# Layer 2's first four token tiles are transposed by VectorE and SBUF transfers instead of TensorE

## The reference

```
x = layernorm(x + attn(x))        # layer 1
x = layernorm(x + ffn(x))         # layer 2

attn:  up = x @ up_w.T;  delta = x @ gate_w.T - local_point
       out = up @ local_approx_output.T
       for m in 1..6: out += (exp(m*log|delta| - c[m]) * sign/keep * up) @ fuse_weight[m].T
       out += (silu(x @ ffn_gate_w.T) * (x @ ffn_up_w.T)) @ ffn_down_w.T      # F = 1248
ffn:   h = silu(x @ q(w1).T) * (x @ q(w2).T);  out = h @ q(w3).T              # H = 1376
q(w) = NF4 quantisation and dequantisation in blocks of 64: w / absmax, nearest of 16 codes, * absmax
```

## Time and profile before

| | us |
|---|---|
| median of 3 runs (range) | 411.65 (411.63 to 411.87) |
| profiled execution, whole | 412.71 |
| its span, first to last instruction | 410.8 |
| TensorE busy in it | 401.8 |
| VectorE, GpSimd, ScalarE busy | 325.1, 290.1, 267.4 |

### The profile page before, as it was taken

One profiled execution on the slowest core, in us unless ns is written; L12 is line 12 of the kernel. 1 busy time (PEld: TensorE's weight loads), 2 busy tenths in 40 slices (PEclk: granted clock), 3 DMA queues, 4 the chain that ended last, 5 costly groups with the idle time before them and its releaser, 6 DMA issues.

```text
span 410.8 us, 5355 instructions
## 1 busy us (share of the span) xinstructions
PE 401.8 (98%) x1770; PEld 327.9 (80%) x1770; DVE 325.1 (79%) x383; ACT 267.4 (65%) x372; POOL 290.1 (71%) x228
## 2 busy tenths in 40 slices
PE   7999999999999999999999999999999999999993
PEld 5888888888877888888888888888888877888872
DVE  3629989779888986999998799987779989935035
ACT  5575666677676847466956658888769777732613
POOL 0077998877978489936993366799999998954430
PEclk9999999999999999999999999999999999999998
DMA  7994101100204362103043000000000000000202
GB/s 258 409 408 146 53 14 51 28 26 0 53 3 123 89 224 69 27 0 104 1 131 146 0 2 1 2 0 0 2 2 0 2 0 0 2 0 2 102 0 102
DMA packets 10042, 26.48 MB, mean 64 GB/s; under 512 B 1248, under 2 KB 1632, under 8 KB 9760
## 3 DMA queue, kind: packets, MB, share of 16 engines
q1 hardware_dynamic: 9584, 25.37, 18.2%
q10 hardware_dynamic: 432, 0.79, 0.7%
HBM read 24.06 MB, written 2.10 MB: 64 GB/s over the span
## 4 chain that ended last, share of the span: by engine, by line
PE 95%; DMA 2%; DVE 1%; ACT 0%; issue 0%; POOLq 0%; SPq 0%; DVEq 0%; ACTq 0%
PE PS L1257 32%; PE PS L1258 31%; PE PS L1259 31%; DMA h<-xT 2%; PE PS L1361 1%; POOLq L249 0%; SPq L522 0%; ACT R L567 0%; DVE stats L933 0%; DVE R L928 0%; DVE x_lo L1041 0%; ACT x_hi L567 0%; ACT std L784 0%; DVE mv L959 0%; DVE std L972 0%
## 5 line engine op out<-in xcount | busy, mean ns | idle before, releaser
L1182 POOL TENSOR_SCALAR level<-side 128x1024 f32<-128x1024 int8 (+2 forms) x119 | 129.7, 1090 | 27.1 <-ACT side L567 13.0
L855 DVE TENSOR_TENSOR PS<-PS,level 128x1024 f32<-128x1024 f32 (+2 forms) x102 | 120.1, 1178 | 23.1 <-POOL level L1182 19.1
L1257 PE MATMUL PS<-x_hi,w_hi 128*128 128x512 f32 (+1 forms) x348 | 135.8, 390 | 0.9 <-DVE x_lo L1041 0.9
L1259 PE MATMUL PS<-x_hi,w_lo 128*128 128x512 f32 (+1 forms) x348 | 135.6, 390 | 0.0
L1258 PE MATMUL PS<-x_lo,w_hi 128*128 128x512 f32 (+1 forms) x348 | 135.5, 389 | 0.0
L567 ACT ACTIVATE side<-Q 128x1024 int8<-128x1024 f32 (+2 forms) x84 | 80.1, 997 | 17.2 <-DVE PS L851 15.2
L1257 PEld LDWEIGHTS PS<-x_hi,w_hi 128*128 128x128 f32 (+1 forms) x348 | 64.5, 185 | 16.1 <-issue 1.7
L1212 POOL TENSOR_TENSOR l_lo<-h,l_hi 128x512 fp32r<-128x512 f32 (+1 forms) x42 | 57.6, 1379 | 27.3 <-ACT l_hi L567 26.4
L1259 PEld LDWEIGHTS PS<-x_hi,w_lo 128*128 128x128 f32 (+1 forms) x348 | 64.5, 185 | 14.5
L1258 PEld LDWEIGHTS PS<-x_lo,w_hi 128*128 128x128 f32 (+1 forms) x348 | 64.5, 185 | 14.4
L1257 PE MATMUL PS<-x_hi,l_hi 128*128 128x512 f32 x144 | 56.1, 390 | 0.0
(11 more groups left out here) (100 smaller groups left out, 510.6 us busy)
## 6 DMA issues: line engine op xcount, KB each, us to landing
Q<-w SPq DMA_DIRECT2D x10, 512.0 KB, 13.8
raw<-w_in SPq DMA_DIRECT2D x9, 512.0 KB, 12.3
raw<-w_out SPq DMA_DIRECT2D x14, 256.0 KB, 2.6
raw<-w SPq DMA_DIRECT2D x5, 512.0 KB, 3.8
R<-xN SPq DMA_DIRECT2D x2, 1024.0 KB, 5.4
raw<-w_fuse SPq DMA_DIRECT2D x7, 256.0 KB, 2.6
out<-R SPq DMA_DIRECT2D x7, 256.0 KB, 2.0
h<-xT SPq DMA_DIRECT2D x2, 512.0 KB, 8.1
```

Of the source, the lines that this page charges most:

```text
L855: v.tensor_tensor(total, total, level_of(s), ALU.add).then_inc(s_add, 1)
L1182: g.tensor_scalar(level_of(s), side_of(s), LIMITS[k][1], LIMITS[k][0], ALU.min, ALU.max).then_inc(s_level, 1)
L1257: t_.matmul(dst, a_hi, b_hi, start=start, stop=False)
L1259: return t_.matmul(dst, a_lo, b_hi, start=False, stop=stop)
```

## The change

- TensorE no longer transposes tiles 0 to 3 (16 of its 32 transposes). `transpose_x` stays for tiles 4 to 7.
- VectorE's new `turn_x(t)` transposes tile t in squares of 32x32, from R to part of h (SBUF to SBUF), for all four tiles at x = 7. Part of h that holds nothing yet is used: `x_squares` and `x_back`.
- SyncE then issues 16 transfers inside SBUF that put the squares in their places, for all four tiles together: each is 32 partitions by 4x128 elements, 64 KB. They stand behind the load of x's second half and ahead of the loads of w3.
- ScalarE splits tiles 0 to 3 out of `x_back` in SBUF, at x = 12 and 13 (before: out of PSUM, at 8 and 10).
- The low parts of tiles 0 to 3 are GpSimd's, at x = 12 and 13 (before: VectorE's, at 8 and 10). `pair(2, 0)` waits for them (`s_xl_first`).
- `turn_nf4(0)`, the transpose of the first quantised unit into the PSUM banks that the transposes used, waits for the first pass's banks (`s_y`) instead of `s_xl`.
- `SHARE` is dealt anew for all three engines.

```diff
@@ -217,22 +217,22 @@
 SHARE = {
     "scalar": [
...
-        3, 0, 0, 0, 0, 0, 0, 0, 1, 1, 1, 0, 1, 0, 0, 0, 0, 0, 0, 0, 0, 0, 0, 1, 0, 2, 0, 1, 0, 0, 0, 0, 3, 0,
+        3, 0, 0, 0, 0, 0, 1, 2, 1, 0, 1, 0, 0, 0, 0, 0, 0, 0, 0, 0, 0, 0, 0, 1, 0, 1, 0, 2, 0, 0, 0, 0, 4, 0,
...
@@ -290,6 +290,11 @@
+        h_first = h[:].rearrange("p (f a n) -> p f a n", f=C2, a=2)[:, :, 0, :]
+        x_squares, x_back = h_first[:, 0:TILES, :], h_first[:, TILES:2 * TILES, :]
@@ -339,7 +344,7 @@
         s_fact = sem("s_fact")
-        s_xh, s_xl = sem("s_xh"), sem("s_xl")
+        s_xh, s_xl, s_xl_first = sem("s_xh"), sem("s_xl"), sem("s_xl_first")
         s_whi, s_wlo0, s_wlo = sem("s_whi"), sem("s_wlo0"), sem("s_wlo")
         s_whi4, s_wlo4 = sem("s_whi4"), sem("s_wlo4")
@@ -353,6 +358,7 @@
         s_centred, s_root = sem("s_centred"), sem("s_root")
+        s_xsq, s_xback = sem("s_xsq"), sem("s_xback")
         s_xtr, s_turn, s_w3turn = sem("s_xtr"), sem("s_turn"), sem("s_w3turn")
         s_max, s_floor, s_prep, s_nrm = sem("s_max"), sem("s_floor"), sem("s_prep"), sem("s_nrm")
@@ -444,6 +450,21 @@
+        def x_turned(t):
+            if t < TILES:
+                return x_back[:, t, :].rearrange("p (a c i) -> p c a i", a=P // SQ, c=DC)
+            return PS[:, XT_BANK + t % 2, :].rearrange("p (c a i) -> p c a i", c=DC, a=P // SQ)
+        def x_part(x, t):
+            return x[:, :, t * P:(t + 1) * P].rearrange("p c (a i) -> p c a i", i=SQ)
+        def wait_x_turned(eng, t):
+            if t < TILES:
+                eng.wait_ge(s_xback, 16 * (P // SQ) ** 2)
+            else:
+                eng.wait_ge(s_xtr, t - TILES + 1)
             return XT_BANK + c % 2
@@ -544,6 +565,12 @@
+            sp.wait_ge(s_xsq, TILES)
+            for q in range(P // SQ):
+                for a in range(P // SQ):
+                    sp.dma_start(x_back[q * SQ:(q + 1) * SQ, :, a * P:(a + 1) * P],
+                                 x_squares[a * SQ:(a + 1) * SQ, :, q * P:(q + 1) * P]).then_inc(s_xback, 16)
             for k in range(W3_UNITS):
                 if u < UNITS - 1:
@@ -673,13 +700,12 @@
                 beside()
-                act.wait_ge(s_xtr, t + 1)
+                wait_x_turned(act, t)
                 if t < TILES:
                     act.wait_ge(s_tile, TT)
-                copy(x_hi[:, :, t * P:(t + 1) * P],
-                     PS[:, XT_BANK + t % 2, :].rearrange("p (c t) -> p c t", c=DC)).then_inc(s_xh, 1)
+                copy(x_part(x_hi, t), x_turned(t)).then_inc(s_xh, 1)
                 beside()
@@ -742,8 +768,8 @@
                         scale_and_shift(1, 0)
-                    if x in (8, 10):
-                        for t in (x - 8, x - 7):
+                    if x in (12, 13):
+                        for t in (2 * x - 24, 2 * x - 23):
                             split_x(t)
                         split_nf4((x - 12) // 2)
@@ -971,23 +997,31 @@
+            def turn_x(t):
+                beside()
+                dve.wait_ge(s_norm, t + 1)
+                if t == 0:
+                    dve.wait_ge(s_llo_h, C1)
+                v.transpose(x_squares[:, t, :].rearrange("p (q c i) -> p c q i", q=P // SQ, c=DC),
+                            R[:, t, :].rearrange("p (c q j) -> p c q j", c=DC, q=P // SQ)).then_inc(s_xsq, 1)
                 dve.wait_ge(s_xh, X_PARTS + t + 1)
-                if t < TILES:
-                    wait_job_done(dve, PLACE[1, ("fuse", 3)])
-                else:
-                    dve.wait_ge(s_tile, TT)
-                v.tensor_tensor(x_lo[:, :, t * P:(t + 1) * P],
-                                PS[:, XT_BANK + t % 2, :].rearrange("p (c t) -> p c t", c=DC),
-                                x_hi[:, :, t * P:(t + 1) * P].bitcast(F32), ALU.subtract).then_inc(s_xl, 1)
+                dve.wait_ge(s_tile, TT)
+                v.tensor_tensor(x_part(x_lo, t), x_turned(t), x_part(x_hi, t).bitcast(F32),
+                                ALU.subtract).then_inc(s_xl, 1)
-                if f in (0, 2):
-                    dve.wait_ge(s_xl, X_PARTS + (TILES if f == 0 else TT))
+                if f == 0:
+                    dve.wait_ge(s_y, TILES)
+                elif f == 2:
+                    dve.wait_ge(s_xl, X_PARTS + TT - TILES)
                 else:
                 v.transpose(turned(f).rearrange("p (s n i) -> p n s i", s=2, i=SQ),
@@ -1096,9 +1130,9 @@
                         normalise(1, 0)
-                    if x in (8, 10):
-                        for t in (x - 8, x - 7):
-                            lo_x(t)
+                    if x == 7:
+                        for t in range(TILES):
+                            turn_x(t)
                     if x == 10:
                     if x in (12, 14):
@@ -1211,6 +1245,13 @@
+            def lo_x(t):
+                beside()
+                pool.wait_ge(s_xh, X_PARTS + t + 1)
+                wait_job_done(pool, PLACE[1, ("fuse", 3)])
+                g.tensor_tensor(x_part(x_lo, t), x_turned(t), x_part(x_hi, t).bitcast(F32), ALU.subtract).then_inc(
+                    s_xl_first, 1)
                 dst, k = h_of(2, i), multiplied(i, True) - 1
@@ -1239,6 +1280,9 @@
                     lo_raw(JOB[1, AGAIN[(5, 9, 10, 11, 12).index(x)]])
+                if i == 1 and x in (12, 13):
+                    for t in (2 * x - 24, 2 * x - 23):
+                        lo_x(t)
             for i in range(2 * C2):
                     gate_times_up(i)
@@ -1301,7 +1345,10 @@
                         pe.wait_ge(*bank_free(i - 2))
-                    pe.wait_ge(s_xl, X_PARTS + (TILES if half == 0 and i < 2 else TT))
+                    if half == 0 and i < 2:
+                        pe.wait_ge(s_xl_first, TILES)
+                    else:
+                        pe.wait_ge(s_xl, X_PARTS + TT - TILES)
                 project(layer, slot, 0, half, bank, m)
@@ -1354,8 +1401,8 @@
                 if t % TILES >= 2:
-                    pe.wait_ge(s_xl, X_PARTS + t - 1)
-                elif t >= TILES:
+                    pe.wait_ge(s_xl, X_PARTS + t - 1 - TILES)
+                else:
                     pe.wait_ge(s_wlo4, 2)
                     last = t_.transpose(PS[:, XT_BANK + t % 2, c * P:(c + 1) * P], R[:, t, c * P:(c + 1) * P], ident[:])
@@ -1403,11 +1450,7 @@
             for n in range(PASS_START[1], PASS_START[2] - TAILS[1]):
-                x = n - PASS_START[1]
-                stage2(n, {4: (s_h, 2 * C1), 6: (s_y, 1), 7: (s_y, 2)} if x == 0 else {})
-                if x in (7, 9):
-                    transpose_x(x - 7)
-                    transpose_x(x - 6)
+                stage2(n, {4: (s_h, 2 * C1), 6: (s_y, 1), 7: (s_y, 2)} if n == PASS_START[1] else {})
             stage2_end(1)
                 pair(2, i)
```

## The result

| | before | changed |
|---|---|---|
| median of 5 runs each, us | 411.69 | 420.26 |
| lowest to highest | 411.63 to 412.45 | 419.83 to 420.40 |
| ratio, 95% interval | | 1.0204 (1.0192 to 1.0215) |
| profiled execution, whole (span) | 412.71 (410.8) | 420.4 (418.5) |

The change makes the kernel 8.6 us slower. The forecast was 411.9 with a range to 413.5. Lines moved: L821 is now L847 (`rcp`), L855 is L881, L851 is L877, L858 is L884, L831 is L857 (maxima of w3), L928 is L954 (the adds of tiles 4 and 5), L947 is L973, L981 is L1014, L1002 is L1036, L1173 is L1207, L1182 is L1216, L1212 is L1246, L1257 to L1259 are L1301 to L1303, L1361 is L1408. The low parts of x on GpSimd are L1252, the turns L1007, the transfers of squares L572.

What follows compares the result with a forecast made beforehand. TensorE was taken as the bound, with GpSimd a quarter of a microsecond behind. Transposes saved (-1.76) plus the wait at out 4 (+2.05) gave +0.3, so 411.9 us from 411.65, range 409.9 to 413.5.

Steps and rivals of the forecast that it cites:

- What the transposes take: TensorE's two groups of eight transposes, at 195.02 and 201.62: 0.88 us each, a gain of at most 1.76 us.
- GpSimd's stretch and the wait at out 4: GpSimd from out 7's low part to the end of out 4's: 17.7 us, making TensorE wait 2.05 us at out 4.
- S: Start of out 7's low part on GpSimd: 197.26 before, forecast 197.35, range 196.4 to 198.5.
- VectorE's turns: VectorE's four transposes of tiles 0 to 3 in squares: 4 x 0.71 us, done at 197 to 198.5.
- the lock-out: GpSimd's row of two-input operations shuts VectorE's `rcp` out until near 216.5; `pair(2, 0)` waits 5.4 us; about 417; chance 0.12.
- The second rival: VectorE locked out at `rcp` by GpSimd's 12 two-input operations in a row: about 417 us, chance 0.12.
- The upstream wait: Redealt steps put a 1.2 us VectorE add before a scaled low part, stalling TensorE: 412.5 to 413.5, chance 0.08.
- The transfers: SyncE's 16 issues at 0.43 us, landing 4.0 later at 208 to 209.4, covered by 1 to 2.5 us.

## Why the prediction was wrong, step by step

**What the transposes take: right in size, wrong in worth.** 0.88 us a group is what the rows gave, and doubling them cost 1.8 us for 1.76. The step "every microsecond taken from TensorE's queue is a microsecond of the kernel, as long as its operands come that much earlier" had its condition, and the text then went on to "a gain or loss here reaches the end". That holds for a loss. For a gain the medians of the kernel with a quarter of the transposes show 0.0 of 1.3 us.

**GpSimd's stretch and the wait at out 4: right.** Forecast 17.7 us from S to the end of out 4's low part; measured 215.54 - 198.02 = 17.52. The low part of x in four pieces took 1.25 from start to start, as taken. S was 198.02 against 197.35, in the range of its own (196.4 to 198.5), partly because all came 0.7 late from upstream. The waits at out 7 and out 4 cost 1.85 for 2.05, and this part of the sum came out at 1.00 - 0.73 = +0.27 for a forecast of +0.3.

**VectorE's turns: right.** 2.65 for four, 0.71 each at most.

**The failing step: the chance of the lock-out.** The second rival was the case, with the mechanism, the place and nearly the price: `rcp` held until GpSimd waits for it, "near 216.5", measured 216.84; 9.4 us later than before, measured 9.75; time 417, measured 420.26. I gave it 0.12, because "L947 did get in, so the boundaries are not all shut". One boundary that let an operation through was read as a rule for all. `rcp` itself, in the same view, had been let in at neither of two boundaries and been let go at the pause ahead of the level, and that was the nearer row: same operation, same neighbours. In the change it was let in at none of 12 boundaries. With that reading the rival was the likeliest case.

**Its price was 3 us short.** The tile adds came 7.1 us late; the forecast wait of 5.4 was 4.24, since TensorE itself came 1.0 later. Not in it were the matmuls at the low clock behind a long wait (1.6), the waits in the fuse jobs (1.4) and those for tiles 4 to 7 (0.6).

**The upstream wait, given 0.08, also came**, with +1.36 for a forecast of 0.6 to 1.6. It came from the new table: with the old one it was gone, in both kernels that had it. These rivals are not exclusive, and the range treated them as if one at most would come. This is why the range fails even without the lock-out: the kernel with the other form of `rcp` takes 415.48, for this wait and for the loads of w3, which the sum had no term for.

**The transfers: priced only as far as their landing.** The 16 issues took 0.65 each for a forecast of 0.43, the landing 2.0 for 4.0, and the two errors nearly cancel: ScalarE could split at 210.03 for a forecast of 210.5. "SyncE's queue holds nothing else there" was wrong for what stands behind: the loads of w3 moved from 207.08 to 208.63, and without the lock-out that is the next thing VectorE waits for (1.5 us for half of the transfers). In the changed kernel it is covered by the lock-out, which holds VectorE longer.

The loss of 8.6 us in the measured steps: 4.8 the lock-out with its slow matmuls, 1.5 the loads of w3 behind the transfers, and 2.3 left. The trace of the kernel with neither (the other form of `rcp`, half of the transfers) accounts for the rest. Its last matmul is 2.0 us behind the one of the kernel before, loading taken out: 1.4 upstream, 0.3 up to out 4 (1.76 of transposes saved, 2.1 lost again) and 0.3 at tiles 4 to 7. The place near 240 us was not tried alone.

## What to carry to other kernels

Count the unbroken rows of one engine's operations, not only its busy time: where GpSimd and VectorE work side by side, a small VectorE operation of a form that was once held between two GpSimd operations may be held to the end of the row, and taking out the one different operation that made a pause can cost more than its own length. Before work is taken off the busiest engine, take some of it away without giving it to anybody, and see whether the time falls; here 1.3 us less gave nothing in the medians, a warning that could have been had before the change was built. A transfer costs its queue as well as its data: see what is issued next behind it, and who waits for that.

## What the hardware showed that I had not expected

- **A hold over many operations.** VectorE's clamp on 128x32 numbers took 0.18 us with GpSimd idle, 1.56, 3.11 and 5.56 behind parts of a row of two-input operations, and 15.56 behind 13 of them. In the changed kernel, in the one before and in four others (one level put back, the level taken away, low parts behind out 4, old table) it ended 0.03 to 0.05 us after GpSimd's last operation had, with nothing running there. The forms held beside it were `tensor_scalar` and products of two SBUF inputs on 128x4 and 128x2 numbers (0.36 to 1.47 for 0.16 or 0.17); reciprocals, transposes into PSUM and maxima ran through. Why the statistics at 189.97 were let in at a boundary inside a row, in both kernels, and `rcp` at none, stays open.
- **The clock after a wait.** Behind waits of 2.18 us (out 4, one level put back), 3.76, 4.08 and 5.13 us the matmuls ran at a pitch of 0.43 for eight to fourteen in a row. Of six waits of over 1 us that ended in transposes (1.40, 1.41, 1.69, 1.74, 2.85 and 2.86 us), those of 1.74 and 2.86 were followed by nine and seven slow matmuls, the others by none: 2.85 and 2.86 differ in that, so the length of the wait doesn't decide it. Eight matmuls at 0.43 for 0.227 are 1.6 us on top of the wait. When a wait brings them and when not, these runs don't tell.
- **Transfers inside SBUF.** 64 KB of 32 partitions are issued in 0.65 us each on SyncE's queue, where a load of 192 KB took 0.43, and land after 2.0 us in the median, where the nearest small loads took 4.0.
